# State-space layer with expert FFN: GpSimd takes other products, TensorE adds two of them, and the gathers of a unit are parted

## The chip, the cores and the metric

The kernel runs on one core of one Trainium2 chip. The metric is the device time of one launch in microseconds (us); the kernel before has a median of 2426.65 us over three runs (2425.75 to 2430.33). Names of engines: PE is TensorE (PEld its weight loads), DVE is VectorE, ACT is ScalarE, POOL is GpSimd, SP is the queue that issues most DMAs.

## The reference

For 32 samples of 512 rows by 256 features (fp32): normalise each row to `xn`, and return x + attn(xn) + ffn(xn). The attention part is a selective scan, the other a mixture of 8 experts, each of which picks the 128 rows of a sample with the highest gate:

```
deltaBC = xn @ W_deltaBC.T ; delta, B, C = split(64 | 16 | 16)
delta = softplus(delta @ W_dt.T + b_dt)
h_n[t] = exp(delta[t]*A_n) * h_n[t-1] + delta[t]*B_n[t]*xn[t]     # 16 states n, 256 channels
y[t] = sum_n h_n[t]*C_n[t] + D*xn[t]
S = softmax(xn @ Wg.T) per row; G, I = top_k(S per expert, 128)
out[I] += G * (gelu(xn[I] @ W1[e] + b1[e]) @ W2[e] + b2[e])       # 8 experts a sample
```

## The kernel before

After an opening of some 190 us (layer norm, projections, gates, the picks of the experts) comes the main part. It is written as five instruction streams, one for each engine, that wait for one another on semaphores. Nothing but the order written in these streams sets the order of the work; each engine takes its instructions strictly in turn.

A *sample* b has 16 *steps* s, one for each state n. A step n is, on DVE: the scan of 128x1024 (two halves of 256 channels by 512 rows), the multiply of the next step, `bx` (du times B of state n+1, into `bank_x`, L936), and the *product* of the scan with C_n (L1008), into one of the four buffers `prod[:, n % 4]`. POOL adds the products one after the other into `ysum` (L585); this is called sum n. Two products of a sample are made by POOL in place of DVE (L573): product 4 (the scan wrote to `state`, which is `zabs`; POOL writes `prod` and adds it), and product 8, which stays in a buffer of its own, `kept`, and isn't added by POOL. `ysum`, `kept` and `skip` (D times x) are turned by PE through the identity matrix and added in PSUM (`y_rows`, L1110), in two halves, each of four places with three terms; then ACT copies the half to `yrow` and POOL writes it to `out` with an adding DMA (`add_y`, L554).

B of a state has to be spread over all partitions in `bank_b`, one bank of PSUM that holds one state. For n = 3 and 0 (mod 4) PE does it with a matmul (L1116), for n = 1 and 2 (mod 4) ACT copies it from `b_wide` (L748). Each waits until DVE's `bx` of the step before has read the bank.

The experts' work is cut into 128 *units* u (two sets of 128 picked rows each), four to a sample; unit u runs beside slot u % 4 of the sample, that is beside four steps. In its unit u PE runs, in positions q = 0 to 7: the up matmuls of unit u+1 at q = 0 to 3 (L1163), at q = 3 ahead of them the turning of the gathered rows of unit u+2 (`chosen_columns`, L1082, which waits for the DMAs), at q = 4 to 7 the down matmuls of unit u (L1229), and the spreads of B at q = 4 and 6. The first half of a y is turned at q = 5 of slot 0 of the sample behind it, the other at q = 1 of slot 3. ACT does the gelus, the scaling by the gate (`og`, L757), the copies of turned rows, and eight decays exp(delta*A_n) a unit.

POOL also issues the indirect DMAs. In unit u at its first step (i = 0) it issues both gathers for unit u+3 (`gather`, L509, into `ex[:, (u+3) % 2]`), at i = 1 and 2 the two scatters of unit u-1 (`scatter`, L540). In slot 3 it also adds the two parts of delta and multiplies du for the next sample (`take_delta` L517, `take_du` L523), between sum 12 and the gathers. SP loads C for unit u+1 (`load_c`, L397) once all products of unit u-1 are done, those of DVE and those of POOL.

Of the kernel before, what the change touches and what calls it, by code (L numbers as in the profile page):

```python
# [50 lines left out]
GP_STEPS = (4, 8)  # L51
KEPT = 8
# [26 lines left out]
def build(nc, x, wdbc, wdt, bdt, alog, dpar, wg, w1, b1, w2, b2, out):  # L79
    ctx = ExitStack()  # L80
    with ctx:
# [187 lines left out]
        def sums(s):  # L269

            return s - (s + N - 1) // N - (s + N - 1 - KEPT) // N

        def gp_prods(s):

            return sum((s + N - 1 - n) // N for n in GP_STEPS)

# [4 lines left out]
        def expert_of(u):  # L281

            return u // 8 % E

# [168 lines left out]
        def _(pool):  # L453
# [50 lines left out]
            def gather(u):  # L504

                wait(pool, ex_tr, u - 1)
                pool.wait_ge(picks_done, 2 + u // 64 * 2)
                for i in range(UB):
                    pool.indirect_dma_start(  # L509
                        out=ex[:, u % 2, i], out_offset=None, in_=xn_rows,  # L510
                        in_offset=bass.IndirectOffsetOnAxis(ap=idx_all[:, u * UB + i:u * UB + i + 1], axis=0),
                    ).then_inc(gathered[u % 2], 16)
# [12 lines left out]
            for v in range(2):  # L525
                gather(v)
            take_delta(1, 0)
            take_du(1, 0, 16)
            gather(2)
# [26 lines left out]
            def main(j):  # L556
                for k in range(BU):
# [6 lines left out]
                    for i in range(STEPS):  # L564
                        n = sl * STEPS + i
                        s = b * N + n
                        if there(b, NB):
                            if n in GP_STEPS:
                                pool.wait_ge(scan_done, s + 1)
                                pool.wait_ge(c_in[u % 2], (u // 2 + 1) * 16)  # L570
                                from_, to = (kept[:, m % 2], kept[:, m % 2]) if n == KEPT else (state[:], prod[:, i])
# [4 lines left out]
                            elif s < NB * N - 1:  # L576
                                pool.wait_ge(prod_done, dve_prods(s + 1))
# [6 lines left out]
                            if n > 0 and n != KEPT and s < NB * N - 1:  # L584
# [27 lines left out]
        def _(act):  # L612
# [72 lines left out]
            def take_z(nb, par, dt):  # L685
# [3 lines left out]
                wait(act, gp_prod_done, gp_prods((nb - 2) * N + KEPT) if nb > 1 else 0)  # L689
# [140 lines left out]
        def _(dve):  # L830
# [97 lines left out]
            def multiply_b(s, par, b):  # L928
# [3 lines left out]
                if (s - 2) % N in GP_STEPS:  # L932
# [43 lines left out]
            def main(j):  # L976
                for k in range(BU):
# [5 lines left out]
                    for i in range(STEPS):  # L983
# [5 lines left out]
                        if n == KEPT:  # L989
                            wait(dve, y_tr, b * 2 - 2)  # L990
                            into = kept[:, par].rearrange("p c t -> p (c t)")
                        elif n in GP_STEPS:
# [11 lines left out]
                        if n in GP_STEPS:  # L1004
# [280 lines left out]
```

## Time and profile before

| | |
|---|---|
| median of three runs | 2426.65 us |
| the profiled execution: its time / its span | 2422.32 us / 2420.4 us |
| busy: PE, DVE, ACT, POOL | 2286.8, 2349.7, 2074.3, 2146.5 us |
| granted PE clock, mean | 0.987 of full speed |
| POOL sums L585 | 415 + 32, 2702 and 2374 ns |
| DVE scans L997 / bx L936 / products L1008 | 512 of 2.28 us / 512 of 1206 ns / 448 of 1216 ns |
| POOL products L573 | 32 of 3421 ns (product 4), 32 of 2893 ns (product 8) |
| POOL gathers L509 / scatters L540 | 256 of 1010 ns / 256 of 1601 ns |

The span is cut off 1.9 us short of the execution's own time. The durations of POOL and PE are from the entry into the engine to the end, so those of neighbours overlap; the distance between two starts tells more. A "busy" PE counts matmuls by modelled ends. Times in the sections below are microseconds from the span's start.

### The profile page before, as it was taken

To read this page: it belongs to the slowest core of one execution; us is meant where nothing else is said; L and a number is where in the kernel's file an instruction comes from. 1 tells how busy PE (TensorE), PEld (TensorE's weight loads), DVE (VectorE), ACT (ScalarE), POOL (GpSimd) and SP (SyncE) were. 2 spreads that over 40 slices of the span, in tenths; PEclk is the share of its full clock that TensorE was granted. 3 is DMA by queue.
4 is the path that set the end of the run, shared out by engine and by line. 5 is a ranking of instruction groups with operands and counts; after the bars stand their busy time and mean duration, and the time that the engine had idled before them with its cause. 6 is when DMAs were issued, how large, how long until landed. Compare 5 with 4: busy or idle time off the path is not lost. (4 is left out here: it accounts for less than half of the span.)

```text
span 2420.4 us, 33772 instructions
## 1 busy us (share of the span) xinstructions
PE 2286.8 (94%) x10756; PEld 1816.4 (75%) x10756; DVE 2349.7 (97%) x1975; ACT 2074.3 (86%) x3629; POOL 2146.5 (89%) x1235
## 2 busy tenths in 40 slices
PE   7749999999999999999999999999999999999996
PEld 4437777777777777777777777777778777777775
DVE  5799999999999999999999999999999999999997
ACT  7748889898888888988888889888898989888884
POOL 5527999999999899999999999999999999999997
PEclk9969999999999999999999999999999999999998
DMA  9967575645656565555656555565646456565444
GB/s 344 338 209 266 158 221 157 177 136 148 168 147 173 145 161 141 165 154 134 184 137 173 136 166 145 141 176 143 177 127 180 127 151 163 149 173 139 128 127 79
DMA packets 151649, 403.04 MB, mean 167 GB/s; under 512 B 19536, under 2 KB 88240, under 8 KB 134832
## 3 DMA queue, kind: packets, MB, share of 16 engines
q1 hardware_dynamic: 84208, 316.72, 38.2%
q0 software_dynamic: 66048, 83.92, 20.6%
q8 instruction: 87, 1.43, 0.2%
q14 instruction: 90, 0.74, 0.1%
q10 hardware_dynamic: 1216, 0.23, 0.0%
HBM read 323.72 MB, written 91.75 MB: 172 GB/s over the span
## 5 line engine op out<-in xcount | busy, mean ns | idle before, releaser
L585 POOL TENSOR_TENSOR ysum<-ysum,prod 128x1024 f32<-128x1024 f32 x415 | 1121.4, 2702 | 20.3 <-DVE prod L1008 12.1
L997 DVE TENSOR_TENSOR_SCAN bank_x<-decay,bank_x 128x1024 f32<-128x1024 f32 x448 | 1024.7, 2287 | 8.9 <-DVE bank_x L936 0.5
L1163 PE MATMUL bank_l<-ext,w_sb 128*128 128x256 f32 x4096 | 968.9, 384 | 28.2 <-ACT og L757 22.6
L1229 PE MATMUL bank_l<-w_sb,hid 128*128 128x256 f32 x4096 | 939.0, 382 | 0.0
L1163 PEld LDWEIGHTS bank_l<-ext,w_sb 128*128 128x128 f32 x4096 | 760.3, 191 | 166.5 <-ACT og L757 31.0
L1229 PEld LDWEIGHTS bank_l<-w_sb,hid 128*128 128x128 f32 x4096 | 767.5, 190 | 130.0 <-issue 29.0
L717 ACT ACTIVATE decay<-delta,a_sb 128x511 f32<-128x511 f32 x1024 | 641.9, 707 | 15.8 <-POOL delta L517 14.6
L936 DVE TENSOR_TENSOR bank_x<-du,bank_b 128x1024 f32<-128x1024 f32 x512 | 617.6, 1206 | 4.7 <-ACT bank_b L748 3.2
L726 ACT ACTIVATE hid<-bank_l,b_all 128x256 f32<-128x256 f32 x1024 | 431.5, 475 | 203.8 <-PE bank_l L1163 200.7
L1008 DVE TENSOR_TENSOR prod<-bank_x,c_all 128x1024 f32<-128x1024 f32 x448 | 544.9, 1216 | 0.1
L540 POOL DMA_INDIRECT out<-og,idx_all x256 | 410.0, 1601 | 43.8 <-POOL ysum L585 42.5
L509 POOL DMA_INDIRECT ex<-xn_rows,idx_all x256 | 258.5, 1010 | 109.4 <-issue 61.4
L748 ACT COPY bank_b<-b_wide 128x512 f32<-128x512 f32 x256 | 153.5, 599 | 7.2 <-DVE bank_x L936 6.2
L757 ACT ACTIVATE og<-bank_l,gate_all 128x256 f32<-128x256 f32 x256 | 105.9, 464 | 32.6 <-PE bank_l L1229 32.5
L1116 PE MATMUL bank_b<-bcs,pick 96*128 96x512 bf16 x256 | 98.5, 385 | 31.0 <-DVE bank_x L936 30.0
L717 ACT ACT_TABLE_LOAD x97 | 124.5, 1283 | 1.7
L824 ACT ACT_TABLE_LOAD x95 | 121.9, 1283 | 1.7
L573 POOL TENSOR_TENSOR prod<-zabs,c_all 128x1024 f32<-128x1024 f32 x32 | 109.5, 3421 | 0.0
L1116 PEld LDWEIGHTS bank_b<-bcs,pick 96*128 96x128 bf16 x256 | 24.8, 97 | 99.6 <-DVE bank_x L936 51.7
L573 POOL TENSOR_TENSOR kept<-kept,c_all 128x1024 f32<-128x1024 f32 x32 | 92.6, 2893 | 0.0
L1082 PE MATMUL bank_t<-ident,ex 128*128 128x128 f32 x512 | 77.3, 274 | 9.2 <-DMA ex<-xn_rows,idx_all 9.2
L741 ACT COPY ext<-bank_t 128x512 f32<-128x512 f32 x128 | 76.1, 594 | 6.1 <-PE bank_t L1082 6.1
(117 smaller groups left out, 1958.9 us busy)
## 6 DMA issues: line engine op xcount, KB each, us to landing
c_all<-bc_rows SPq DMA_DIRECT2D x128, 1024.0 KB, 5.1
b_wide<-bc_rows SPq DMA_DIRECT2D x128, 512.0 KB, 4.5
w_sb<-in_w SPq DMA_DIRECT2D x32, 1024.0 KB, 9.3
decay<-in_x SPq DMA_DIRECT2D x32, 512.0 KB, 6.8
xn_rows<-c_all SPq DMA_DIRECT2D x32, 512.0 KB, 6.5
out<-yrow POOLq DMA_DIRECT2D x32, 512.0 KB, 8.5
xr<-xn_rows SPq DMA_DIRECT2D x30, 512.0 KB, 6.0
bc_rows<-prod SPq DMA_DIRECT2D x32, 192.0 KB, 5.1
```

What stands on the lines that cost most here:

```text
L509: pool.indirect_dma_start(out=ex[:, u % 2, i], out_offset=None, in_=xn_rows, in_offset=bass.IndirectOffsetOnAxis(ap=idx_all[:, u * UB + i: ...
L540: pool.indirect_dma_start(out=out_rows, out_offset=bass.IndirectOffsetOnAxis(ap=idx_all[:, w * UB + c:w * UB + c + 1], axis=0), in_=og[:, ...
L573: nc.gpsimd.tensor_tensor(to, from_, c_all[:, u % 2, i][:, None, :].broadcast_to([P, HC, T]), ALU.mult).then_inc(gp_prod_done, 1)
L585: nc.gpsimd.tensor_tensor(ysum[:, m % 2], first, prod[:, i], ALU.add).then_inc(sum_done, 1)
L717: nc.scalar.activation(decay[:, par, i, dt, 1:T], delta[:, dpar_, dt, 1:T], ACT.Exp, scale=a_sb[:, dt, n:n + 1]).then_inc(decay_done, 1)
L726: nc.scalar.activation(hid[:, k % 2, f], bank_l[(pair + k) % 2][:, (f % 2) * UT:(f % 2 + 1) * UT], ACT.Gelu_apprx_tanh, bias=b1_all[:, exp ...
L748: nc.scalar.copy(bank_b[:], b_wide[:, s % STEPS - WIDE[0]]).then_inc(b_ready, 1)
L936: nc.vector.tensor_tensor(bank_x[:, s % 2].rearrange("p (c t) -> p c t", c=HC), du[:, par], bank_b[:][:, None, :].broadcast_to([P, HC, T]) ...
L997: nc.vector.tensor_tensor_scan(into, decay[:, k % 2, i].rearrange("p c t -> p (c t)"), bank_x[:, s % 2], 0.0, ALU.mult, ALU.add).then_inc( ...
L1008: nc.vector.tensor_tensor(prod[:, i], bank_x[:, s % 2].rearrange("p (c t) -> p c t", c=HC), c_all[:, u % 2, i][:, None, :].broadcast_to([P ...
L1163: i = nc.tensor.matmul(bank_l[(q + v) % 2][:, (f % 2) * UT:(f % 2 + 1) * UT], w1_sb[:, e2, hc, f * P:(f + 1) * P], ext[:, v % 2, hc], star ...
L1229: i = nc.tensor.matmul(o, hid[:, w % 2, f, c * K:(c + 1) * K], w2_sb[:, w_par, f], start=False, stop=(f == FC - 1 and c == UB - 1))
```

## The change

Products 4, 13 and 15 are now POOL's (`GP_STEPS`), product 8 goes back to DVE. 13 and 15 are the ones that stay out of the sums, in `kept[:, 0]` and `kept[:, 1]`: `kept` was double-buffered over samples, and has now one buffer for each of the two products, so the scans 13 and 15 wait until both halves of the last sample's y have been turned. PE turns and adds four terms instead of three for each place of a y. In the last sample POOL makes only product 4, and 13 and 15 are DVE's.

The two gathers of a unit are parted: the first stays at step i = 0, the second is issued at i = 3, behind that step's sum or product. The last y is no longer turned at once when everything is there, but in the order skip, ysum, product 13, product 15, each term when it is ready, the second half into `bank_l[0]` instead of `bank_x`. The last two scatters stand at i = 1 and 2 instead of both at i = 2.

```diff
-GP_STEPS = (4, 8)
-KEPT = 8
+GP_STEPS = (4, 13, 15)
+KEPT = (13, 15)
...
+        def by_gp(s):
+            return s % N in GP_STEPS and not (s // N == NB - 1 and s % N in KEPT)
+        def stays(s):
+            return s % N in KEPT and s // N < NB - 1
...
-            def gather(u):
+            def gather(u, i):
                 wait(pool, ex_tr, u - 1)
                 pool.wait_ge(picks_done, 2 + u // 64 * 2)
-                for i in range(UB):
-                    pool.indirect_dma_start(
+                pool.indirect_dma_start(
...
-                            if n in GP_STEPS:
+                            if by_gp(s):
                                 pool.wait_ge(scan_done, s + 1)
                                 pool.wait_ge(c_in[u % 2], (u // 2 + 1) * 16)
-                                from_, to = (kept[:, m % 2], kept[:, m % 2]) if n == KEPT else (state[:], prod[:, i])
+                                from_, to = (kept[:, n // 14], kept[:, n // 14]) if stays(s) else (state[:], prod[:, i])
...
-                        if i == 0:
-                            if there(u + 3, NU):
-                                gather(u + 3)
+                        if i in (0, 3) and there(u + 3, NU):
+                            gather(u + 3, i // 3)
...
-                        if i == 2 and u == NU - 1:
-                            scatter(u, 1)
-                            scatter(u, 0)
+                        if i in (1, 2) and u == NU - 1:
+                            scatter(u, 2 - i)
...
-                        if n == KEPT:
-                            wait(dve, y_tr, b * 2 - 2)
-                            into = kept[:, par].rearrange("p c t -> p (c t)")
+                        if stays(s):
+                            wait(dve, y_tr, b * 2)
+                            into = kept[:, n // 14].rearrange("p c t -> p (c t)")
...
-                        terms = [ysum[:, par, dt, rows], kept[:, par, dt, rows], skip[:, par, dt, rows]]
+                        terms = (ysum[:, par], kept[:, 0], kept[:, 1], skip[:, par])
...
-                        if q in (5, 6) and u == NU:
+                        if q == 5 and u == NU:
...
+                            for half in range(2):
+                                last_term(skip[:, par], half, first=True)
+                            pe.wait_ge(sum_done, sums(NB * N))
+                            for half in range(2):
+                                last_term(ysum[:, par], half)
+                            for n in KEPT:
+                                pe.wait_ge(prod_done, dve_prods((NB - 1) * N + n + 1))
+                                for half in range(2):
+                                    o = last_term(prod[:, n % STEPS], half, last=(n == KEPT[-1]))
```

Where the instructions stand now. First POOL, from sum 12 of a sample (slot 3) to sum 1 of the next; "L585" is a sum, "DMA ex" a gather, "DMA out" a scatter. Before:

```order
L585 TENSOR_TENSOR ysum<-ysum,prod 128x1024 [waits sum_done,prod_done] x2
L517 TENSOR_TENSOR delta<-delta,zabs 128x1024 [waits sp_step]
L523 TENSOR_TENSOR du<-delta,xnt 128x1024 [waits xnt_in0,delta_done,bx_done]
L509 DMA ex<-xn_rows,idx_all 128x256 [waits picks_done,ex_tr]
L509 DMA ex<-xn_rows,idx_all 128x256
L585 TENSOR_TENSOR ysum<-ysum,prod 128x1024 [waits sum_done,prod_done]
L540 DMA out<-og,idx_all 16384x256 [waits scattered00,og_done]
L585 TENSOR_TENSOR ysum<-ysum,prod 128x1024 [waits sum_done,prod_done]
L540 DMA out<-og,idx_all 16384x256 [waits scattered01,og_done]
L585 TENSOR_TENSOR ysum<-ysum,prod 128x1024 [waits sum_done,prod_done]
L509 DMA ex<-xn_rows,idx_all 128x256 [waits ex_tr,picks_done,sum_done,prod_done]
L509 DMA ex<-xn_rows,idx_all 128x256
```

And the same place of the changed kernel ("L594" a sum, "L582 kept" the products 13 and 15, "L516" a gather):

```order
L594 TENSOR_TENSOR ysum<-ysum,prod 128x1024 [waits sum_done,prod_done]
L524 TENSOR_TENSOR delta<-delta,zabs 128x1024 [waits sp_step]
L530 TENSOR_TENSOR du<-delta,xnt 128x1024 [waits xnt_in0,delta_done,bx_done]
L516 DMA ex<-xn_rows,idx_all 128x256 [waits picks_done,ex_tr]
L582 TENSOR_TENSOR kept<-kept,c_all 128x1024 [waits sum_done,c_in1,scan_done]
L549 DMA out<-og,idx_all 16384x256 [waits og_done,scattered00,sum_done,gp_prod_done]
L594 TENSOR_TENSOR ysum<-ysum,prod 128x1024 [waits sum_done,prod_done]
L549 DMA out<-og,idx_all 16384x256 [waits scattered01,og_done]
L582 TENSOR_TENSOR kept<-kept,c_all 128x1024 [waits sum_done,c_in1,scan_done]
L516 DMA ex<-xn_rows,idx_all 128x256 [waits ex_tr,picks_done,sum_done,gp_prod_done]
L516 DMA ex<-xn_rows,idx_all 128x256 [waits ex_tr,picks_done,sum_done,prod_done]
L594 TENSOR_TENSOR ysum<-prod 128x1024 [waits y_tr,prod_done]
```

The second gather of the unit has moved from behind `du` to behind product 15, past two elementwise operations, a sum and two scatters; the next unit's first gather follows it.

Then PE in slot 0 of the next sample, from the turning of the gathered rows to the spread of state 4; its order is the same in both kernels but for the terms of y. Before:

```order
L1082 MATMUL bank_t<-ident,ex 128x128 [waits ext_done,gathered0,xnt_in1]
L1082 MATMUL bank_t<-ident,ex 128x128 x3
L1163 MATMUL bank_l<-ext,w_sb 128x256 [waits gelu_done]
L1163 MATMUL bank_l<-ext,w_sb 128x256 x3
L1116 MATMUL bank_b<-bcs,pick 128x512 [waits bx_done]
L1225 MATMUL bank_l<-b_all,ones 128x512 [waits og_done,gelu_done]
L1229 MATMUL bank_l<-w_sb,hid 128x256 x8
L1110 MATMUL bank_t<-ident,ysum 128x128 [waits gp_prod_done,skip_done,sum_done,ext_done]
L1110 MATMUL bank_t<-ident,kept 128x128
L1110 MATMUL bank_t<-ident,skip 128x128
```

The same in the changed kernel, from the matmul that adds the bias to the spread of state 4 (one of the four places of y; the other three read alike):

```order
L1240 MATMUL bank_l<-b_all,ones 128x512 [waits og_done,gelu_done]
L1244 MATMUL bank_l<-w_sb,hid 128x256 x8
L1114 MATMUL bank_t<-ident,ysum 128x128 [waits gp_prod_done,skip_done,sum_done,ext_done]
L1114 MATMUL bank_t<-ident,kept 128x128 x2
L1114 MATMUL bank_t<-ident,skip 128x128
...
L1114 MATMUL bank_t<-ident,skip 128x128
L1131 MATMUL bank_b<-bcs,pick 128x512 [waits bx_done]
```

Nothing moved here but the four more turns a half; both spreads that DVE needs in slot 0, of states 3 and 4, stand behind the wait for both gathers of the unit (`gathered0`).

## Rows read from the trace of the kernel before

**Rows 1.** Windows: us, PE, PEld, DVE, ACT, POOL busy (x), PEclk, DMA share, GB/s.
```profile
1196.50:1265.90 69.40, 67.76 (x322) 54.68 (x321) 69.10 (x47) 61.74 (x110) 65.03 (x37) 1.00 0.53 140
```

**Rows 2.** Timeline of DVE: start us, us, engine, line, op, out<-in, count.
```profile
1202.63 1.20 DVE L936 TENSOR_TENSOR bank_x<-du,bank_b 128x1024 f32<-128x1024 f32 x1
...
1208.18 1.22 DVE L1008 TENSOR_TENSOR prod<-bank_x,c_all 128x1024 f32<-128x1024 f32 x1
...
1216.11 1.21 DVE L936 TENSOR_TENSOR bank_x<-du,bank_b 128x1024 f32<-128x1024 f32 x1
...
1238.31 1.21 DVE L936 TENSOR_TENSOR bank_x<-du,bank_b 128x1024 f32<-128x1024 f32 x1
...
1240.55 2.27 DVE L997 TENSOR_TENSOR_SCAN zabs<-decay,bank_x 128x1024 f32<-128x1024 f32 x1
1242.74 1.21 DVE L936 TENSOR_TENSOR bank_x<-du,bank_b 128x1024 f32<-128x1024 f32 x1
1244.09 2.30 DVE L997 TENSOR_TENSOR_SCAN bank_x<-decay,bank_x 128x1024 f32<-128x1024 f32 x1
1246.29 1.20 DVE L936 TENSOR_TENSOR bank_x<-du,bank_b 128x1024 f32<-128x1024 f32 x1
...
1309.96 2.27 DVE L997 TENSOR_TENSOR_SCAN zabs<-decay,bank_x 128x1024 f32<-128x1024 f32 x1
```

**Rows 3.** Timeline of POOL, slot 3 into slot 0; in brackets idle time before, releaser.
```profile
1214.74 2.36 POOL L517 TENSOR_TENSOR delta<-delta,zabs 128x1024 f32<-128x1024 f32 x1
...
1221.08 0.98 POOL L509 DMA_INDIRECT ex<-xn_rows,idx_all  x1 [0.31 <-issue]
...
1229.88 2.89 POOL L585 TENSOR_TENSOR ysum<-ysum,prod 128x1024 f32<-128x1024 f32 x1
```

**Rows 4.** Timeline of PE, slot 0 of the next sample.
```profile
1224.43 3.72 PE L1163 MATMUL bank_l<-ext,w_sb 128*128 128x256 f32 x16 [0.97 <-ACT og L757]
1227.99 0.60 PE L1082 MATMUL bank_t<-ident,ex 128*128 128x128 f32 x4
...
1230.69 0.39 PE L1116 MATMUL bank_b<-bcs,pick 96*128 96x512 bf16 x1 [0.38 <-DVE bank_x L936]
...
1234.88 0.27 PE L1110 MATMUL bank_t<-ident,ysum 128*128 128x128 f32 x1
...
1236.19 0.38 PE L1116 MATMUL bank_b<-bcs,pick 96*128 96x512 bf16 x1
```

**Rows 5.** Timeline of ACT: the copy into bank_b for step 6.
```profile
1244.69 0.60 ACT L748 COPY bank_b<-b_wide 128x512 f32<-128x512 f32 x1
```

**Rows 6.** Tile ex: landing of all gathers, 300 to 2340 us.
```profile
DMA to landing us min/median/max: 2.7/2.8/4.2
```

**Rows 7.** Tile ex, 1986.2 to 1986.7 us: one gather beside a load of c_all.
```profile
DMA to landing us min/median/max: 3.2/3.2/3.2
```

**Rows 8.** Timeline of SP: that load of c_all.
```profile
1987.23 0.32 SPq L397 DMA_DIRECT2D c_all<-bc_rows  x1
```

**Rows 9.** Timeline of PE after two longer idle times.
```profile
179.40 0.48 PE L1131 MATMUL bank_x<-ident,hid 128*128 128x128 f32 x1 [4.69 <-DVE hid L942]
...
179.88 3.62 PE L1163 MATMUL bank_l<-ext,w_sb 128*128 128x256 f32 x8
...
1989.60 5.41 PE L1163 MATMUL bank_l<-ext,w_sb 128*128 128x256 f32 x16 [2.20 <-ACT og L757]
```

**Rows 10.** Windows: the second of these places.
```profile
1986.50:1995.00 8.50, 6.30 (x25) 5.00 (x24) 7.84 (x6) 6.07 (x13) 8.15 (x5) 0.80 0.65 202
```

**Rows 11.** Timeline of PE: first turn of the last y.
```profile
2405.80 0.45 PE L1110 MATMUL bank_t<-ident,ysum 128*128 128x128 f32 x1 [8.91 <-DVE prod L1008]
```

**Rows 12.** Timeline of POOL: last sum and last write of y.
```profile
2402.09 2.34 POOL L585 TENSOR_TENSOR ysum<-ysum,prod 128x1024 f32<-128x1024 f32 x1 [0.46 <-DVE prod L1008]
...
2413.10 1.36 POOL L554 DMA_DIRECT2D out<-yrow  x1 [5.12 <-DVE yrow L1015]
```

More of the change, by code:

```diff
@@ L269, in sums @@
         def sums(s):
-            return s - (s + N - 1) // N - (s + N - 1 - KEPT) // N
+            return s - (s + N - 1) // N - sum((s + N - 1 - n) // N for n in KEPT)
         def gp_prods(s):
-            return sum((s + N - 1 - n) // N for n in GP_STEPS)
+            return sum((s + N - 1 - n) // N for n in GP_STEPS) - sum(s > (NB - 1) * N + n for n in KEPT)
         def dve_prods(s):
@@ L525, in _ @@
             for v in range(2):
-                gather(v)
+                for i in range(UB):
+                    gather(v, i)
             take_delta(1, 0)
             take_du(1, 0, 16)
-            gather(2)
+            for i in range(UB):
+                gather(2, i)
             split_rest(NG - 1)
@@ L575, in main @@
                                 pool.wait_ge(gp_prod_done, gp_prods(s + 1))
-                            elif s < NB * N - 1:
+                            elif n not in KEPT:
                                 pool.wait_ge(prod_done, dve_prods(s + 1))
@@ L583, in main @@
                                 first = ysum[:, m % 2]
-                            if n > 0 and n != KEPT and s < NB * N - 1:
+                            if n > 0 and n not in KEPT:
                                 nc.gpsimd.tensor_tensor(ysum[:, m % 2], first, prod[:, i], ALU.add).then_inc(sum_done, 1)
@@ L688, in take_z @@
                 wait(act, delta_done, nb - 1)
[L689 removed]
+                wait(act, gp_prod_done, gp_prods((nb - 2) * N + KEPT[0]) if nb > 1 else 0)
                 wait(act, du_done, nb - 2)
@@ L1097, in y_ready, with y_rows, last_term @@
                 pe.wait_ge(skip_done, y + 1)
-            def y_rows(par, half, last=False):
-                into = bank_x[:, 0, 0:T] if last and half else bank_t[:]
+            def y_rows(par, half):
                 for c in (2 * half, 2 * half + 1):
                     for dt in range(HC):
-                        part = into[:, (c % 2) * D + dt * P:(c % 2) * D + (dt + 1) * P]
+                        part = bank_t[:, (c % 2) * D + dt * P:(c % 2) * D + (dt + 1) * P]
                         rows = slice(c * P, (c + 1) * P)
-                        terms = [ysum[:, par, dt, rows], kept[:, par, dt, rows], skip[:, par, dt, rows]]
-                        if last:
-                            terms.append(prod[:, STEPS - 1, dt, rows])
+                        terms = (ysum[:, par], kept[:, 0], kept[:, 1], skip[:, par])
                         for t, term in enumerate(terms):
-                            o = nc.tensor.matmul(part, term, ident[:], start=(t == 0), stop=(t == len(terms) - 1), is_transpose=True)
+                            o = nc.tensor.matmul(part, term[:, dt, rows], ident[:],
+                                                 start=(t == 0), stop=(t == len(terms) - 1), is_transpose=True)
                 o.then_inc(y_tr, 1)
+            def last_term(term, half, first=False, last=False):
+                into = bank_l[0] if half else bank_t[:]
+                for c in (2 * half, 2 * half + 1):
+                    for dt in range(HC):
+                        o = nc.tensor.matmul(into[:, (c % 2) * D + dt * P:(c % 2) * D + (dt + 1) * P],
+                                             term[:, dt, c * P:(c + 1) * P], ident[:],
+                                             start=(first and c % 2 == 0 and dt == 0), stop=(last and c % 2 == 1 and dt == HC - 1), is_transpose=True)
+                return o
             def spread_b(s, n, par):
```

22 lines of the change are left out of this document (11 added, 11 removed).

## The prediction, written before the changed kernel ran

> **What bounds the kernel now.** I read the page first: DVE is busy for 97% of the span, PE for 94%, POOL for 89%. Then the windows of one sample in the middle [rows 1]: in 69.40 us DVE is busy for 69.10, PE for 67.76, POOL for 65.03, ACT for 61.74. So DVE sets the pace of 69.4 us a sample (two scans of step 4 are 69.41 apart [rows 2]), but PE and POOL have little to spare, and what counts is who waits for whom when one of them is moved. For this I read the timelines of DVE, POOL and PE over one sample, side by side [rows 2 to 4].
>
> DVE: a step is a scan, the bx of the next step and a product. Three steps with products take 1216.11 - 1202.63 = 13.48 us [rows 2], about 4.45 each. Step 4, whose product is POOL's, takes from scan to scan 1244.09 - 1240.55 = 3.54 [rows 2]. A product given away is therefore worth 0.9 us, not its 1.22: the next scan must then wait for the bx right in front of it.
>
> POOL runs behind DVE. The product of step 12 is ready at 1208.18 + 1.22 = 1209.40 [rows 2], and sum 12 ends when `take_delta` starts, at 1214.74 [rows 3]; sum 15 ends at 1229.88 + 2.89 = 1232.77, though DVE began the bx of step 15 at 1216.11. Nothing suffers, since four `prod` buffers lie between them.
>
> PE runs ahead of POOL. In slot 0 of the next sample it turns the gathered rows at 1227.99 [rows 4], before POOL has ended sum 15. The rows that it turns there are those of the unit three after the one in slot 3: POOL issued the second of their gathers at 1221.08 [rows 3], and with 2.8 us to landing [rows 6] they are there at 1223.9, 4.1 us early. Behind this turning stand PE's spreads of states 3 and 4, without which DVE cannot go on: that of state 4 ends at 1236.19 + 0.38 = 1236.57 [rows 4], and DVE's bx of step 4 starts at 1238.31 [rows 2], 1.74 later.
>
> **The change, part by part.** *DVE:* one product fewer in each sample but the last (15 products there against 14 before). At 0.9 us that would be 28 us less over 31 samples.
>
> *POOL:* one product more, one sum fewer. The elementwise operations are as many as before and as long (2.9 us for sum and product 8 alike where they follow another instruction), and the pause of 0.31 us between two gathers goes [rows 3]. POOL's work a sample stays at 65 us, below any pace that can come out here. I cost it at nothing; the order is what costs.
>
> *PE:* eight more turns a sample. Twelve take from 1234.88 to 1236.19 [rows 4], 0.11 each, so 0.9 us a sample, 0.44 of it ahead of the spread of state 4.
>
> *The parted gathers:* this is the term that decides. In slot 3 the second gather moves from behind `take_du` to behind product 15. PE needs it in the unit right after. The route from DVE to POOL to PE and back to DVE is a loop of one sample, and its length is a lower bound of the pace:
>
> 1. From the ready product 12 to the end of sum 12: 2.4 us (a sum alone is 2.34 [rows 12]).
> 2. From there to the end of product 15: before, 1214.74 to 1232.77, 18.03 us [rows 3]; one gather less in between, 0.98 + 0.31; so 16.7. POOL does this without waiting for anybody, and it cannot start earlier than DVE's product 12.
> 3. Second gather to the start of the turning: 0.3 for the pause ahead of it, landing 3.2, semaphore and weight load 0.3; 3.8 us. The landing is a choice. All gathers lie between 2.7 and 4.2 us with a median of 2.8 [rows 6]. But SP's `load_c` for slot 1 waits for product 15 too, so its 1024 KB are issued in the same moment as this gather. The nearest case is one whose gather had such a load issued 1.0 us after it (1987.23 against 1986.2 [rows 8]): 3.2 us [rows 7]. I take that, and 2.8 and 4.2 as the ends.
> 4. PE from the first turn to the end of the spread of state 4: 1236.57 - 1227.99 = 8.58, less 0.38 that it waited there for DVE [rows 4], plus the four turns, 0.44; 8.6 us.
> 5. To DVE's bx of step 4: 0.1 us. From there to the bx of step 12: before, 1202.63 + 69.41 - 1238.31 = 33.7 [rows 2], plus 0.9 since product 8 is DVE's again; 34.6 us.
> 6. ACT's copy for step 6 ends at 1244.69 + 0.60 = 1245.29 [rows 5], 1.0 us before DVE uses it at 1246.29 [rows 2], and it hangs on the same PE. The slack of the spread of state 4 was 1.74, that of this copy 1.0: closed up to both, DVE loses another 0.7 us.
> 7. From the bx of step 12 to its product: 1209.40 - 1202.63 = 6.8 us [rows 2].
>
> Sum: 2.4 + 16.7 + 3.8 + 8.6 + 34.7 + 0.7 + 6.8 = 73.7 us, with the ends of the landing 73.3 to 74.7. That is longer than the 68.5 that DVE alone would need (69.4 - 0.9). POOL can't shorten it by being less late: steps 1 and 2 already take it to be waiting for product 12.
>
> DMA arbitration bears on step 3. The Trainium skill, page "DMA: Bandwidth & Descriptors", section "Queues, rings and completion order", says that each DMA engine takes turns between the queues for which it has work, a packet at a time. By that the gather is slowed by the load beside it, and the sum would go by the upper end; if the gather had its way free, by the lower. Rows 7 agree weakly, with 0.4 us above the median.
>
> *The clock:* PE arrives at its turning at about 1227.99 - 0.9 on the clock of these rows (it is tied to DVE, which gives up product 13 before), and the gather lands at 1209.40 + 2.4 + 16.7 + 3.5 = 1232.0: PE stands still for some 5 us in each sample. After an idle time of 4.69 us eight matmuls took 3.62 us, and after one of 2.20 us sixteen took 5.41, where sixteen at full speed take 3.72 [rows 9, 4]; the granted clock of that stretch is 0.80 [rows 10], part at 1.2 and part at 2.4 GHz. Each time 1.7 us was lost. In the loop the work behind the idle time is that of term 4, so I add 1.7: 75.4 us a sample.
>
> The Trainium skill, page "TensorE: Matmul & The Clock Gate", section "HAM oscillation — how this bites in real kernels", describes a loop in which a wait for a DMA lets the clock fall again in every turn, so that the price is paid each time and not once. By it the 1.7 us come in every sample; without it the pace would be 73.7. The trace before has no repeated case, so it shows the price and not how often it falls due.
>
> *Other places.* The scan of 13 now waits for both halves of the last y; these are turned at the start of slot 3, steps before, so nothing. `load_c` for slot 1 waits for product 15, but DVE wants that C only at step 4, over 12 us after. The second gathers of slots 0, 1 and 2 also move back behind their step 3, 7 or 11, but POOL, without `take_delta` and `take_du` in those slots, is back at DVE's heels by then; by my estimate PE finds their rows there within about a microsecond of its turning, and the slack of 1.74 us, if theirs is like it, holds that.
>
> *The end:* before, PE starts its 32 turns at 2405.80, when all is ready [rows 11], and POOL writes at 2413.10 [rows 12]. Now skip is turned early, ysum once sum 14 has ended (2402.09 + 2.34 = 2404.4 [rows 12]), and 24 turns follow at about 0.21 us: 2409.6 against 2411.8. With 0.9 for product 8 on DVE, 1 us less.
>
> **Sum.** The turn from slot 3 to slot 0 comes 31 times: 31 x (75.4 - 69.4) = 186 us, less 1. Against the profiled execution's 2422.3 us (its span is 2420.4) that is 2607; the median of the runs lies 4.3 above that execution: **2612 us**.
>
> **The rivals.**
> *The same loop, clock up.* If PE keeps 2.4 GHz through the waits: 31 x 4.3 - 1 = 132, 2559 us. For it: after an idle time of 0.97 us PE is at full pace (3.72 for sixteen at 1224.43 [rows 4]). Against it: the waits here are five times as long.
> *The wait spreads.* The landing at its upper end, 4.2, and the clock low twice, in slot 0 and at one more late gather: 75.4 + 1.0 + 1.7 = 78.1 a sample, 31 x 8.7 - 1, 2695 us. For it: SP's loads and POOL's gathers now start together. Against it: slack of about 1 us elsewhere.
> *The other side: the gather stays hidden and DVE's shorter sample wins.* Its place is the turning in slot 0, its price 31 x 0.9 + 1 = 29 us: 2398 us. It decides if the second gather lands no later than PE can stand, that is within the 1.74 us of the spread of state 4 less 0.44, while I have some 5 us of waiting. For it: no busy share speaks of this wait [rows 1], and PE is 67.76 us busy without it, so it may come to its turning later than I think. Against it: the fixed 19.1 us of terms 1 and 2.
> *PE as the bound.* 67.76 + 0.9 is 68.6 of DVE's 68.5: with its small waits PE would hold the sample at 69.4 and the gain is gone, 2426 us. It needs the gather in time as well.
>
> **How the numbers follow.** Forecast 0.56; clock up 0.20; the wait spreads 0.12; DVE's gain 0.08; PE as the bound 0.04. Of this kernel a difference of 0.2% (5 us) is about what can be told from none. Faster 0.08, within 0.04, slower 0.88. The range takes in the clock-up case with the landing at its lower end (31 x 3.9 - 1 above the median, 2547) and a little below, and goes up to near 2695: 2535 to 2685 leaves out the two cases without the wait and half of the third, 0.18.
>
> **What would show it.** Right: PE idle for about 5 us before L1089 in slot 0 of each sample, released by the DMA into `ex`; DVE idle for some 5 us a sample before the bx of steps 3, 4 or 6, released by PE's spread or ACT's copy; a mean granted clock near 0.97; a sample of 75 us, steps without product still 3.5; the gather beside `load_c` landing in over 3 us; POOL waiting for DVE's products around step 12. Wrong: PE's turning never waits for the gather; then the pace is that of DVE or PE. If the pace is near 73.7 with a clock of 1.0 the clock term is wrong; if POOL never waits for DVE and lags by more, terms 1 and 2 are.

## The result, and the profile after

The changed kernel takes 2722.61 us (median of 4 runs, 2716.91 to 2729.24), 1.122 times the kernel before (95% interval 1.119 to 1.125), whose median beside it was 2426.2 us. It is slower, as forecast, but by 296 us where the forecast had 185: the time lies above the range of 2535 to 2685. One execution of a run below, e7_filled, took 4149 us at a granted clock of 0.57, a slow state of the chip, and is left out of its times (with it the median is 2670.53, and from that come the 52 us in the text of e10).

The page of the changed kernel, its span, the busy times, the granted clock by slices, and three groups of section 5, which answer to the table before the prediction:

```profile
span 2719.3 us, 34359 instructions
PE 2367.1 (87%) x11004; PEld 1883.0 (69%) x11004; DVE 2344.3 (86%) x1945; ACT 2082.9 (77%) x3629; POOL 2142.5 (79%) x1234
...
PEclk9979999999999999999998999999999999998998
...
L594 POOL TENSOR_TENSOR ysum<-ysum,prod 128x1024 f32<-128x1024 f32 x384 | 959.9, 2500 | 322.8 <-DVE prod L1015 317.2
...
L943 DVE TENSOR_TENSOR bank_x<-du,bank_b 128x1024 f32<-128x1024 f32 x512 | 622.6, 1216 | 303.9 <-PE bank_b L1131 200.7
...
L1089 PE MATMUL bank_t<-ident,ex 128*128 128x128 f32 x512 | 94.1, 315 | 258.0 <-issue 234.7
```

Only PE is busy for clearly longer than before (2367 against 2287 us: its added turns, and stretches at a lower clock); DVE, ACT and POOL are within 9 us of their times before, and DVE is down to 86% of the span. DVE's bx now has 303.9 us of idle time in front of it, and PE's turning of the gathered rows (L1089) 258.0. Who waits for whom (engine, line, what it waits for: us in total, times, longest):

```profile
POOL ysum L594 <- DVE prod L1015: 354.9, 225, 7.7
...
PE bank_t L1089 <- issue: 234.7, 80, 8.2
ACT ext L748 <- PE bank_t L1089: 209.8, 65, 8.5
DVE bank_x L943 <- PE bank_b L1131: 200.7, 61, 7.3
DVE bank_x L943 <- ACT bank_b L755: 101.3, 175, 3.5
```

POOL waits for DVE, DVE for PE and for ACT, ACT for PE, and PE for something that the view calls "issue". That PE wait is for a DMA: the instruction waits for the gathers (`gathered0`), the view of its waits names the DMA into `ex` for another 22.9 us, and in the kernel before this place had one single wait (9.2 us, in the opening). One sample of the changed kernel in the windows, from one scan of step 4 to the next:

```profile
1228.65:1307.11 78.46, 70.16 (x330) 56.60 (x329) 68.96 (x46) 62.04 (x109) 64.95 (x35) 0.96 0.55 150
```

It takes 78.46 us where one before took 69.40 [rows 1]; busy times are the same within 0.3 us but for 2.4 us of PE and 1.9 of its weight loads. Now the loop of the prediction, piece by piece, in that sample. DVE:

```profile
1226.38 1.23 DVE L943 TENSOR_TENSOR bank_x<-du,bank_b 128x1024 f32<-128x1024 f32 x1 [1.38 <-PE bank_b L1131]
...
1228.65 2.28 DVE L1004 TENSOR_TENSOR_SCAN zabs<-decay,bank_x 128x1024 f32<-128x1024 f32 x1
...
1262.28 1.20 DVE L943 TENSOR_TENSOR bank_x<-du,bank_b 128x1024 f32<-128x1024 f32 x1
...
1268.02 1.22 DVE L1015 TENSOR_TENSOR prod<-bank_x,c_all 128x1024 f32<-128x1024 f32 x1
...
1298.91 1.23 DVE L943 TENSOR_TENSOR bank_x<-du,bank_b 128x1024 f32<-128x1024 f32 x1 [4.11 <-PE bank_b L1131]
...
1304.84 1.23 DVE L943 TENSOR_TENSOR bank_x<-du,bank_b 128x1024 f32<-128x1024 f32 x1 [1.37 <-PE bank_b L1131]
...
1307.11 2.28 DVE L1004 TENSOR_TENSOR_SCAN zabs<-decay,bank_x 128x1024 f32<-128x1024 f32 x1
```

POOL, from sum 12 to the second gather of slot 3 (what answers to [rows 3]):

```profile
1269.32 2.36 POOL L594 TENSOR_TENSOR ysum<-ysum,prod 128x1024 f32<-128x1024 f32 x1 [1.08 <-DVE prod L1015]
...
1285.55 2.90 POOL L582 TENSOR_TENSOR kept<-kept,c_all 128x1024 f32<-128x1024 f32 x1
1288.73 1.01 POOL L516 DMA_INDIRECT ex<-xn_rows,idx_all  x1 [0.27 <-POOL kept L582]
```

Product 12 is ready at 1268.02 + 1.22 = 1269.24, and sum 12 starts at 1269.32: POOL has caught up with DVE, as terms 1 and 2 had it, and needs 1288.45 - 1269.32 = 19.13 us to the end of product 15 (forecast 19.1). The second gather starts at 1288.73. SP beside it:

```profile
1288.53 0.32 SPq L405 DMA_DIRECT2D c_all<-bc_rows  x1
1288.90 0.45 SPq L346 DMA_DIRECT2D rank<-bc_rows  x1
1289.40 0.58 SPq L412 DMA_DIRECT2D b_wide<-bc_rows  x1
1290.02 0.44 SPq L313 DMA_DIRECT2D w_sb<-in_w  x1
1290.50 0.47 SPq L317 DMA_DIRECT2D w_sb<-in_w  x1
```

In 2 us SP issues the 1024 KB of `c_all`, the rank rows, 512 KB of `b_wide`, and in this sample two loads of weights. The load of `c_all` waits for product 15, and the others stand behind it in SP's stream. And PE (what answers to [rows 4]):

```profile
1294.76 1.09 PE L1089 MATMUL bank_t<-ident,ex 128*128 128x128 f32 x4 [5.71 <-issue]
1295.64 3.01 PE L1178 MATMUL bank_l<-ext,w_sb 128*128 128x256 f32 x8
...
1304.42 0.38 PE L1131 MATMUL bank_b<-bcs,pick 96*128 96x512 bf16 x1
```

PE starts its turning 6.03 us after the gather, and goes on below its full pace: four turns in 1.09 us, where they took 0.60 before [rows 4], and eight matmuls in 3.01, where e10 below has 1.89. The spread of state 4 ends at 1304.80, and DVE's bx of step 4 starts at 1304.84.

### The profile page after: what moved, and what is told of

The parts are those of the page before. It is cut to its first block and busy times, and to the rows that moved or that the text cites. A ratio compares the mean times of both kernels' runs of the same rounds, so it can differ in the third digit from the quotient of the medians.

```text
span 2719.3 us, 34359 instructions
## 1 busy us (share of the span) xinstructions
PE 2367.1 (87%) x11004; PEld 1883.0 (69%) x11004; DVE 2344.3 (86%) x1945; ACT 2082.9 (77%) x3629; POOL 2142.5 (79%) x1234
## 5 line engine op out<-in xcount | busy, mean ns | idle before, releaser
L594 POOL TENSOR_TENSOR ysum<-ysum,prod 128x1024 f32<-128x1024 f32 x384 | 959.9, 2500 | 322.8 <-DVE prod L1015 317.2
L1178 PE MATMUL bank_l<-ext,w_sb 128*128 128x256 f32 x4096 | 999.7, 394 | 28.6 <-ACT og L764 22.1
L1004 DVE TENSOR_TENSOR_SCAN bank_x<-decay,bank_x 128x1024 f32<-128x1024 f32 x418 | 956.2, 2288 | 11.4 <-DVE bank_x L943 1.0
L1178 PEld LDWEIGHTS bank_l<-ext,w_sb 128*128 128x128 f32 x4096 | 792.0, 199 | 167.1 <-ACT og L764 30.5
L943 DVE TENSOR_TENSOR bank_x<-du,bank_b 128x1024 f32<-128x1024 f32 x512 | 622.6, 1216 | 303.9 <-PE bank_b L1131 200.7
L1015 DVE TENSOR_TENSOR prod<-bank_x,c_all 128x1024 f32<-128x1024 f32 x418 | 509.1, 1218 | 0.1
L516 POOL DMA_INDIRECT ex<-xn_rows,idx_all x256 | 260.1, 1016 | 76.0 <-DVE gate_all L956 21.7
L1089 PE MATMUL bank_t<-ident,ex 128*128 128x128 f32 x512 | 94.1, 315 | 258.0 <-issue 234.7
L1089 PEld LDWEIGHTS bank_t<-ident,ex 128*128 128x128 f32 x512 | 65.9, 159 | 296.3 <-issue 277.1
L748 ACT COPY ext<-bank_t 128x512 f32<-128x512 f32 x128 | 75.2, 587 | 239.2 <-PE bank_t L1089 209.8
L582 POOL TENSOR_TENSOR kept<-kept,c_all 128x1024 f32<-128x1024 f32 x62 | 163.8, 2642 | 0.6
L1004 DVE TENSOR_TENSOR_SCAN kept<-decay,bank_x 128x1024 f32<-128x1024 f32 x62 | 141.3, 2280 | 4.1 <-ACT decay L724 3.8
L594 POOL TENSOR_TENSOR ysum<-prod 128x1024 f32<-128x1024 f32 x32 | 74.9, 2340 | 37.7 <-DVE prod L1015 37.7
```

Source lines behind the costliest of these rows:

```text
L516: pool.indirect_dma_start(out=ex[:, u % 2, i], out_offset=None, in_=xn_rows, in_offset=bass.IndirectOffsetOnAxis(ap=idx_all[:, u * UB + i: ...
L582: nc.gpsimd.tensor_tensor(to, from_, c_all[:, u % 2, i][:, None, :].broadcast_to([P, HC, T]), ALU.mult).then_inc(gp_prod_done, 1)
L594: nc.gpsimd.tensor_tensor(ysum[:, m % 2], first, prod[:, i], ALU.add).then_inc(sum_done, 1)
L943: nc.vector.tensor_tensor(bank_x[:, s % 2].rearrange("p (c t) -> p c t", c=HC), du[:, par], bank_b[:][:, None, :].broadcast_to([P, HC, T]) ...
L1004: nc.vector.tensor_tensor_scan(into, decay[:, k % 2, i].rearrange("p c t -> p (c t)"), bank_x[:, s % 2], 0.0, ALU.mult, ALU.add).then_inc( ...
L1015: nc.vector.tensor_tensor(prod[:, i], bank_x[:, s % 2].rearrange("p (c t) -> p c t", c=HC), c_all[:, u % 2, i][:, None, :].broadcast_to([P ...
```

## The experiments

The theories. A: the second gather of slot 3 closes a loop POOL - gather - PE - DVE of one sample. B: the products are the cost, three on POOL or one `kept` buffer each. C: the gather lands late because SP's loads start at the same moment. D: each slot's parted gather costs its share. E: the clock falls in the wait. F and G, on what bounds e1_together, came later and stand with e8_copy_first. Ratios are against the kernel before, run on the same chip beside each group; its median was 2421 to 2423 us there, and 2426 beside the changed kernel, so a difference in us against the changed kernel holds to some 5 us.

**e1_together: both gathers at i = 0.**

```diff
-                        if i in (0, 3) and there(u + 3, NU):
-                            gather(u + 3, i // 3)
+                        if i == 0 and there(u + 3, NU):
+                            gather(u + 3, 0)
+                            gather(u + 3, 1)
```

> The changed kernel with both gathers of a unit back at step i = 0; the products 4, 13, 15, the single kept buffers and the new end stay. Theory A (the second gather behind product 15 closes a loop POOL - gather - PE - DVE of one sample): the loop is gone, the pace is DVE's 68.5 to 69.4 us a sample, 2398 to 2430 us. Rival B (the three products on POOL or the single kept buffers are the cost): it stays above 2600 us.

Measured: 2412.44 us, ratio 0.9968 (0.9956 to 0.9981). The whole loss is the parting; products, `kept` buffers and end together gain 0.3%. Rival B falls. One of its samples, 69.04 us:

```profile
1200.50:1269.54 69.04, 68.19 (x330) 55.68 (x329) 68.05 (x46) 61.81 (x109) 65.05 (x36) 1.00 0.54 140
```

**e2_part_only: the kernel before, gathers parted.**

```diff
-            def gather(u):
+            def gather(u, parts=range(UB)):
...
-                for i in range(UB):
+                for i in parts:
...
-                        if i == 0:
-                            if there(u + 3, NU):
-                                gather(u + 3)
+                        if i in (0, 3) and there(u + 3, NU):
+                            gather(u + 3, (i // 3,))
```

> The kernel before with the gathers parted as in the changed one, and nothing else. Here load_c doesn't wait for a POOL product at the end of slot 3, so the gather has no load beside it. Theory A with theory C (the landing was slow because SP's loads start at the same moment): 2.4 + 16.7 + 3.4 + 8.2 + 33.8 + 0.7 + 6.8 = 72.0 us a sample, with the clock term 1.4 it is 73.4, so 2427 + 31 x 4.0 = 2551 us. If the landing is slow without the loads too: 76 us a sample, about 2630. Rival B: 2427 us.

Measured: 2712.59 us, ratio 1.120 (1.116 to 1.124). Parting alone does as much as the whole change. The size was not as expected (2551, or about 2630 with a slow landing), and its samples are uneven, most from 75 to 82 us. The second gather of slot 3 in two neighbouring samples, POOL:

```profile
1133.32 1.01 POOL L509 DMA_INDIRECT ex<-xn_rows,idx_all  x1 [0.16 <-issue]
...
1213.99 1.00 POOL L509 DMA_INDIRECT ex<-xn_rows,idx_all  x1 [0.16 <-issue]
```

PE's turning that waits for it:

```profile
1141.28 1.09 PE L1081 MATMUL bank_t<-ident,ex 128*128 128x128 f32 x4 [8.29 <-issue]
...
1217.90 0.63 PE L1081 MATMUL bank_t<-ident,ex 128*128 128x128 f32 x4 [3.96 <-issue]
```

And SP around them:

```profile
1132.65 0.33 SPq L404 DMA_DIRECT2D b_wide<-bc_rows  x1
1133.02 0.43 SPq L305 DMA_DIRECT2D w_sb<-in_w  x1
1133.50 0.48 SPq L309 DMA_DIRECT2D w_sb<-in_w  x1
...
1208.74 0.32 SPq L397 DMA_DIRECT2D c_all<-bc_rows  x1
...
1213.60 0.33 SPq L404 DMA_DIRECT2D b_wide<-bc_rows  x1
```

In the first sample two loads of weights (2048 KB) start 0.3 us before and 0.2 us after the gather, and PE starts 7.96 us after the gather; in the second there are only `b_wide`'s 512 KB, 0.4 us before the gather, with `c_all` 5.3 us before it, and it is 3.91. Over the samples 4 to 30 the mean is 7.5 us in the 13 that have loads of weights near the gather, and 4.0 in the other 14. So this kernel, free of `load_c` at that moment, runs into the next loads that SP has, in every second sample.

**e3_slot3_together: parted in slots 0, 1 and 2 only.**

```diff
-                        if i in (0, 3) and there(u + 3, NU):
-                            gather(u + 3, i // 3)
+                        if i == 0 and there(u + 3, NU):
+                            gather(u + 3, 0)
+                        if i == (0 if sl == 3 else 3) and there(u + 3, NU):
+                            gather(u + 3, 1)
```

> The changed kernel, but in slot 3 both gathers at i = 0; in slots 0, 1 and 2 they stay parted. Theory A (only the turn from slot 3 to slot 0 costs): within 15 us of e1_together. Rival D (each of the four parted gathers costs its share): three quarters of the loss stays, about 2650 us.

Measured: 2563.22 us, ratio 1.057 (1.055 to 1.059). Both were wrong. The other slots cost 151 us against e1_together, where A had them free and D wanted about three quarters of the loss. PE waits there too:

```profile
PE bank_t L1091 <- issue: 116.0, 76, 3.2
```

**e6_slot3_only: parted in slot 3 only.**

```diff
-                        if i in (0, 3) and there(u + 3, NU):
-                            gather(u + 3, i // 3)
+                        if i == 0 and there(u + 3, NU):
+                            gather(u + 3, 0)
+                        if i == (3 if sl == 3 else 0) and there(u + 3, NU):
+                            gather(u + 3, 1)
```

> The changed kernel with the gathers parted in slot 3 only; in slots 0, 1 and 2 both stand at i = 0. It is the other half of e3_slot3_together. Theory A (one loop of a sample through the turn of slot 3 to slot 0, in which the waits of the other slots lie in slack): the pace of the changed kernel stays, 78 to 79 us a sample, 2690 to 2722 us. Rival D (the slots add up): 2722 less the 151 us that e3_slot3_together loses against e1_together, 2571 us.

Measured: 2703.23 us, ratio 1.116 (1.114 to 1.117), mean clock 0.949. The one place in slot 3 makes nearly the whole loss, and the two halves don't add up (+0.119 and +0.061 against e1_together, together +0.125). D falls: the waits of the other slots cost 151 us when they are alone (e3), and 16 to 19 us on top of the loop: the changed kernel is at 2722.61, and the two intervals lie apart. Those 19 us are its uneven samples. In the trace of e6 the 31 samples take 78.45 us in the mean and none more than 79.1; in the changed kernel, where the other slots are parted too, it is 79.05, with single ones of 80.7 to 82.5. The mean clock is the same, 0.949 and 0.948.

**e4_load_held: no load beside the gather of slot 3.**

```diff
                 held(gp_prod_done, gp_prods((u - 1) * STEPS))
+                if u > 1 and u % SLOTS == 1:
+                    held(ex_tr, min(u + 2, NU))
```

> The changed kernel, with SP holding the load of c_all for slot 1 (and what is queued behind it, rank and b_wide) until PE has turned the gathered rows in slot 0. Theory C: the gather lands in 3 instead of 5.8 us, the pace falls by 2.8 us a sample, 31 x 2.8 = 87: 2636 us. If the landing has another cause, or the held loads are late themselves: 2722 us or more.

Measured: 2612.01 us, ratio 1.081 (1.077 to 1.084), 110 us less than the changed kernel, or 100 by the ratios. The expectation had 87, with 2.8 us a sample; from gather to turning it fell from 6.20 to 2.88 us in the mean of 31 samples, by 3.3, which is 103. A turning in slot 0, whose gather started 2.81 us before it:

```profile
1017.89 0.70 PE L1091 MATMUL bank_t<-ident,ex 128*128 128x128 f32 x4 [2.59 <-issue]
```

The clock has a part in this run too: in 9 of the first 30 samples PE goes on at full pace from its turning, in this one after an idle time of 3.38 us:

```profile
569.24 0.63 PE L1091 MATMUL bank_t<-ident,ex 128*128 128x128 f32 x4 [3.38 <-issue]
569.71 1.89 PE L1180 MATMUL bank_l<-ext,w_sb 128*128 128x256 f32 x8
```

**e9_slot3_held: e6 and e4 in one.** One loop, no neighbours, no load beside the gather.

```diff
+                if u > 1 and u % SLOTS == 1:
+                    held(ex_tr, min(u + 2, NU))
...
-                        if i in (0, 3) and there(u + 3, NU):
-                            gather(u + 3, i // 3)
+                        if i == 0 and there(u + 3, NU):
+                            gather(u + 3, 0)
+                        if i == (3 if sl == 3 else 0) and there(u + 3, NU):
+                            gather(u + 3, 1)
```

> e6_slot3_only (gathers parted in slot 3 only) with SP's load of c_all for slot 1 held until PE has turned the rows in slot 0, so that one loop and no neighbour is left and its gather has no load beside it. Theories A and C: the landing falls from 5.8 to 2.8 us, the pace from 78.5 to 75.5 us a sample, 2703 - 31 x 3.0 = 2610 us. If e4_load_held gained through something in the other slots: 2650 or more.

Measured: 2601.17 us, ratio 1.074 (1.072 to 1.076); 75.2 us a sample in the mean. The gather, the load that now follows, and PE:

```profile
1241.49 1.02 POOL L518 DMA_INDIRECT ex<-xn_rows,idx_all  x1 [0.27 <-POOL kept L584]
```

```profile
1245.05 0.32 SPq L407 DMA_DIRECT2D c_all<-bc_rows  x1
```

```profile
1244.33 0.63 PE L1093 MATMUL bank_t<-ident,ex 128*128 128x128 f32 x4 [4.52 <-issue]
1244.80 3.42 PE L1182 MATMUL bank_l<-ext,w_sb 128*128 128x256 f32 x8
...
1254.14 0.38 PE L1135 MATMUL bank_b<-bcs,pick 96*128 96x512 bf16 x1
```

2.84 us from gather to turning, where the changed kernel has 6.03 (2.86 and 6.20 in the mean): theory C holds for slot 3. PE still loses pace: eight matmuls in 3.42 us.

**e7_filled and e10_slot3_held_filled: PE kept busy in the wait,** in the changed kernel (44 turns) and in e9_slot3_held (24 turns).

```diff
-            def chosen_columns(k, count, taken):
-
+            def chosen_columns(k, count, taken, fill=0):
+
+                wait(pe, ext_done, taken)
+                for _ in range(fill):
+                    nc.tensor.transpose(bank_t[:, 0:P], ident[:], ident[:])
                 pe.wait_ge(gathered[k % 2], count)
-                wait(pe, ext_done, taken)
...
-                            chosen_columns(v + 1, ((v + 1) // 2 + 1) * 32, v + 1)
+                            chosen_columns(v + 1, ((v + 1) // 2 + 1) * 32, v + 1, 44 if sl == 0 and b > 0 else 0)
```

> The changed kernel, with 44 more turns of the identity (0.11 us each, 4.8 us) in PE's stream ahead of the wait for the gathers in slot 0, so that PE is not idle there. They add nothing to the output. Theory E (the clock falls in the wait and costs 1.35 us behind it in every sample): the clock is near 1.0 and the time is 31 x 1.35 = 42 us less, 2680 us. If the clock costs nothing: 2722 us; if the added turns delay PE: more.

> e9_slot3_held with 24 turns of the identity (2.6 us) ahead of PE's wait in slot 0. The loop as the prediction summed it, with the landing at its lower end and without the clock term: 73.3 us a sample, 2427 + 31 x 3.9 - 1 = 2547 us. If the clock term is worth what e7_filled gained (52 us): 2610 - 52 = 2558 us. If the wait is too short now for the clock to fall: as e9_slot3_held.

Measured: e7_filled 2666.3 us (median of three), ratio 1.100 (1.098 to 1.102), clock 0.983 against 0.948, 56 us less than the changed kernel, or 54 by the ratios; e10 2558.63 us, ratio 1.057 (1.055 to 1.059), clock 0.984 against 0.961, 43 us less than e9. PE in e7, in one of 8 samples of 31 in which the clock still falls: the 44 turns leave 2.17 us of idle time, and the pace behind it is low (eight matmuls in 3.30):

```profile
1272.19 4.97 PE L1087 MATMUL bank_t<-ident 128*128 128x128 f32 x44
1279.33 0.66 PE L1091 MATMUL bank_t<-ident,ex 128*128 128x128 f32 x4 [2.17 <-DMA ex<-xn_rows,idx_all]
1279.82 3.30 PE L1180 MATMUL bank_l<-ext,w_sb 128*128 128x256 f32 x8
```

In the other 23 it doesn't fall, as here, with 2.11 us of idle time:

```profile
1588.98 0.66 PE L1091 MATMUL bank_t<-ident,ex 128*128 128x128 f32 x4 [2.11 <-DMA ex<-xn_rows,idx_all]
1589.48 1.89 PE L1180 MATMUL bank_l<-ext,w_sb 128*128 128x256 f32 x8
```

And in e10, where they leave 1.90:

```profile
1221.94 2.78 PE L1091 MATMUL bank_t<-ident 128*128 128x128 f32 x24
1226.62 0.66 PE L1095 MATMUL bank_t<-ident,ex 128*128 128x128 f32 x4 [1.90 <-DMA ex<-xn_rows,idx_all]
1227.12 1.89 PE L1184 MATMUL bank_l<-ext,w_sb 128*128 128x256 f32 x8
...
1234.78 0.38 PE L1137 MATMUL bank_b<-bcs,pick 96*128 96x512 bf16 x1
```

Eight matmuls in 1.89 again (so in 24 of 31 samples), and from the first turn to the end of the spread of state 4 1235.16 - 1226.62 = 8.54 us; in e9 1254.52 - 1244.33 = 10.19. The clock costs 1.65 us a sample there. Theory E holds: 1.65 is the 1.7 of the prediction, and more than the 1.35 that was expected of e7.

**e5_second_at_1 and e8_copy_first: is there something to gain?**

```diff
-                        if i in (0, 3) and there(u + 3, NU):
-                            gather(u + 3, i // 3)
+                        if i in (0, 1) and there(u + 3, NU):
+                            gather(u + 3, i)
```

> The changed kernel with the second gather at step i = 1 instead of i = 3 (in slot 3 it stands behind product 13, not behind product 15). Theory A: it moves by about 2.5 us against e1_together and is still there before PE turns, and no load of c_all starts in that moment, so no loop. POOL, which in e1_together never waited for DVE's products in the middle of the run and so sets its 69.05 us a sample, loses the 0.3 us pause between gathers four times a sample and gains 0.16 each: 68.5 us a sample, 2412 - 31 x 0.5 = 2396 us. If POOL isn't the bound of e1_together: 2412. If parting as such costs: above 2500.

e8_copy_first is e5 with this in addition:

```diff
+                    early = sl == 0 and 0 < u < NU
+                    if early:
+                        spread_b(u * STEPS + WIDE[0])
                     if there(v - 2, NU) and v - 2 < NU - 1:
                         scale_og(v - 2)
...
-                        if there(u, NU) and pair in (0, 2):
+                        if there(u, NU) and pair in (0, 2) and not (early and pair == 0):
```

> e5_second_at_1, with ACT's copy into bank_b for step 1 of a sample moved ahead of the scaling of og in slot 0. e1_together and e5_second_at_1 have the same pace, 69.05 us a sample, though POOL has less to do in e5; DVE waits 0.76 us a sample, for this copy. Theory F (DVE's wait for the copy is the last thing in the way): the wait goes, 68.3 us a sample, 2410 - 31 x 0.7 = 2388 us. Rival G (a loop of PE and ACT through slot 3 sets the pace, and the og that comes 0.6 us later lengthens it): 2410 us or up to 20 more.

Measured: e5_second_at_1 2410.28 us, ratio 0.9953 (0.994 to 0.9966); e8_copy_first 2409.32 us, ratio 0.9943 (0.9929 to 0.9956). Both beat both kernels, by half a per cent against the one before, but neither gained what its first theory expected: the pace stays at 69.05 to 69.1 us a sample, as in e1_together, and their intervals overlap. A second gather that comes 2.4 us or one operation later does no harm at all. POOL was not the bound of e1_together, and DVE's wait for ACT's copy was a symptom. Most of it goes in e8, from 24.1 us in e1 (23.9 in e5),

```profile
DVE bank_x L944 <- ACT bank_b L756: 24.1, 33, 1.9
```

to 8.4 in e8, and the time stays:

```profile
DVE bank_x L946 <- ACT bank_b L755: 8.4, 31, 2.3
```

Nearest to rival G: in the sample of e1_together shown above PE is busy for 68.19 of 69.04 us. That PE with its small waits sets this pace is argued from that row, not shown.

## Why the prediction was right or wrong

**The mechanism was right.** It needed the gather of slot 3 behind product 15, PE's turning behind it, and the two spreads behind that; e1, e2 and e6 show that this one gather carries all of the loss but some 19 us. Lined up with the sum, in the sample shown:

| term | forecast | changed kernel, this sample |
|---|---|---|
| 1, 2: product 12 ready to product 15 ended | 19.1 | 1288.45 - 1269.24 = 19.2 |
| 3: gather issued, landed, PE starts | 3.8 | 1294.76 - 1288.45 = 6.3 |
| 4: PE to the spread of state 4, with the clock term | 8.6 + 1.7 | 1304.80 - 1294.76 = 10.0 |
| 5, 6: bx of step 4 to bx of step 12 | 34.7 + 0.7 | 1262.28 - 1226.38 = 35.9 |
| 7: bx of step 12 to product 12 | 6.8 | 1269.24 - 1262.28 = 7.0 |
| sum | 75.4 | 78.4 |

**The step that failed is term 3, the landing.** I took 3.2 us, 4.2 for the upper end, and 0.3 for the semaphore and the weight load; it was 6.03 us from the gather to PE's start in this sample, 5.48 to 7.22 over all, 6.20 in the mean. With 2.5 us it is most of the 3.0 missing in this sample. (No row had the 0.3: in e9, where the gather is alone, it is 2.84 us from its issue to PE's start with everything in it.) I had seen that `load_c` would start in the same moment, and priced it by a gather beside which a load started 1.0 us later [rows 7, 8], when a third of that gather's 3.2 us had passed. The rank rows and `b_wide` were left out of the reckoning, though they are queued behind `load_c` on SP and so wait for product 15 as well; the weights, left out too, matter little here: 6.4 us in the mean of 13 samples that have them, 6.0 in 14 that don't. e9 against e6 measures the term by itself: 2703 - 2601 = 102 us or 3.3 a sample. My value for it came from no row with the loads already under way.

The remaining 0.5 us in the table is DVE's waits for ACT's copies, somewhat more than term 6 (0.7). The mean of all 31 samples is (2650.24 - 199.59) / 31 = 79.05, 0.6 above this one; the 0.6 are samples of 80 to 82 us between many of 78.4, which e6 does not have. They belong to a second step, below.

**The clock term was right:** 1.7 us a sample forecast, 1.65 between the PE rows of e9 and e10, and 54 / 31 = 1.7 gained in e7 (1.5 between the mean samples of the two traces, with the clock not wholly kept up). PE was idle for 5.7 us in the sample shown and 6.4 in the mean, where I had said some 5; DVE's idle time before its bx came to 303.9 / 31 = 9.8 us a sample, where I had said 5 too. In each of the first 30 samples of the changed kernel the piece from PE's first turn to the spread of state 4 took 9.8 us or more, against 8.54 at full pace. Here the rule of the Trainium skill (page "TensorE: Matmul & The Clock Gate", section "HAM oscillation — how this bites in real kernels") that the price recurs with every wait agrees: the mean clock is 0.948, and 0.983 where the wait is filled. The forecast of near 0.97 was too high.

**The loop by itself was right.** e10 is the sum without contention and, nearly, without the clock: forecast 73.3 us a sample and 2547 us, measured (2484.43 - 200.68) / 31 = 73.7 and 2558.6. Its samples at full pace take 73.3 us, most of them; those in which the clock fell make up the rest. That 2558.6 is also the number of the rival "clock up", 2559, is chance: that rival had the loads beside the gather.

**"Other places" was wrong.** I gave the gathers of the other slots up to a microsecond that slack would hold, and put them at nothing. e3 shows 116 us of waits and 151 us of time. The slack of the spread of state 4 said nothing of PE's own: PE had hardly any. In the changed kernel most of it is hidden behind the loop, but not all: e6, without it, is 19 us or 0.6% faster. The rival "the wait spreads" (2695) came nearest to the time. Of its two causes the landing went past its upper end of 4.2, and the waits did spread to other slots; a second fall of the clock they did not bring, as the mean clock with and without them (0.948 and 0.949) shows.

**The end.** e1_together needs 2410.7 - 2344.63 = 66.1 us from its last scan of step 4 to the end of the span, against 2420.4 - 2353.74 = 66.7 before (both timelines): 0.6 us less, with one product more on DVE; forecast 1. In the changed kernel this piece is 69.1, with waits of 0.71 and 3.49 us for ACT's copies in its last sample, so there the end gained nothing.

**DVE's gift came to little.** A skipped product saves 0.9 us by scan distances (the three steps of 13.48 us are 4.49 each, not 4.45, so 0.95); but without the loop the sample shrank by 0.35 us only, 69.4 to 69.05. The rival "PE as the bound" had that at nothing and was the nearest to it.

## What to carry to other kernels

Before a DMA is issued later in an engine's stream, follow its consumer: if that engine runs ahead of the issuing one, add up the loop back to the issuer, since it can be longer than any engine's busy time. Price its landing with everything on the other queues that the same event releases: here it came to 6 us, where the median and a case in which the other transfer came later said 3. Add what the clock takes back behind a wait that recurs. And a wait that looks harmless alone can be hidden by a longer one: halves of an edit need not add up (+0.119 and +0.061 made +0.125 here).

## What the runs showed of the hardware that was not expected

A gather of 128 rows of 1 KB takes 2.8 us to its consumer when alone (2.81 in e4, 2.84 in e9), 3.9 with 512 KB issued 0.4 us before it and 1024 KB 5.3 us before (e2), 6.0 with 1024 + 512 KB and the rank rows issued from 0.2 us before to 0.7 after it (the changed kernel, two loads of weights 1.3 us and more after it adding little), and 8.0 with 512 KB issued 0.7 us before and 2048 KB of weights within 0.3 us (e2). The Trainium skill (page "DMA: Bandwidth & Descriptors", section "Queues, rings and completion order") has the DMA engines take turns between queues packet by packet; the order of these four does not speak against that, and I had given it only 0.4 us of weight. How much of the wait is turn-taking no run here shows.

The length of PE's idle time does not by itself say whether the clock falls. Idle times of 4.52 us (e9) and 2.17 (e7) were followed by a lower pace, and so were all 31 waits of 5.15 to 8.22 us in slot 0 of the changed kernel; those of 1.90 (e10), 2.11 (e7) and 3.38 (e4) were not. In e10 a wait of 1.91 us was followed by eight matmuls in 3.35 us, and one of 1.90 by eight in 1.89. What sets these apart is not shown.
